# Two turns of layer-norm rows and one of combine weights done one head later in the second mixer

## What is computed

```python
x = x + L0_attn(layernorm(x))      # 16-head delta rule with short convolutions
x = x + L0_ffn(layernorm(x))       # 8 experts, top 2, plus a shared expert
x = x + L1_attn(layernorm(x))      # 16 query heads on 2 key/value heads, rotary, soft-capped, causal
x = x + L1_ffn(layernorm(x))       # 16 experts, top 6, combine weights from a softmax router
```

```python
logits = SOFTCAP * jnp.tanh((q @ k.T) * SCALE / SOFTCAP)
scores = jax.nn.softmax(jnp.where(causal, logits, -1e30), axis=-1)
out = scores @ v                   # then out @ Wo, added over the heads
```

## Time and profile before

| | |
|---|---|
| median of three runs | 869.14 us (868.95 to 869.23) |
| the profiled execution's own time | 869.01 us |
| its span (first to last instruction) | 867.2 us |
| TensorE matmul busy | 813.6 us, 94% of the span |
| VectorE busy | 456.9 us, 53% |
| ScalarE busy | 318.4 us, 37% |
| POOL busy | 161.9 us, 19% |
| mean granted TensorE clock | 0.988 |

### The profile page before, as it was taken

How to read it: one execution, slowest core, us unless ns; L and a number is a source line. 1 busy time by engine, 2 the same in 40 slices (tenths; PEclk the granted TensorE clock), 3 DMA queues, 4 the chain that set the end, 5 groups by cost and what they waited for, 6 DMA issues and landing times.

```text
span 867.2 us, 12754 instructions
## 1 busy us (share of the span) xinstructions
PE 813.6 (94%) x4543; PEld 568.6 (66%) x4543; DVE 456.9 (53%) x1054; ACT 318.4 (37%) x651; POOL 161.9 (19%) x256
## 2 busy tenths in 40 slices
PE   6979799889899977999999999998999999999998
PEld 3567566666567765677777776776766655555567
DVE  5999766757422225866464666476543252322223
ACT  3987777555033322443323243332312211111111
POOL 3652744113500070111111111111100000000000
PEclk9998999999999997999999999999999999999999
DMA  4002860281253230023010100100224344354431
GB/s 139 2 2 40 264 231 2 52 224 55 98 173 107 74 91 12 19 61 92 25 37 25 37 25 27 35 25 25 63 79 128 112 129 125 122 148 131 130 107 48
DMA packets 63957, 72.07 MB, mean 83 GB/s; under 512 B 14200, under 2 KB 48504, under 8 KB 63896
## 3 DMA queue, kind: packets, MB, share of 16 engines
q1 hardware_dynamic: 59048, 64.06, 24.8%
q0 software_dynamic: 1536, 4.20, 1.5%
q10 hardware_dynamic: 3312, 3.02, 1.0%
HBM read 55.45 MB, written 14.75 MB: 81 GB/s over the span
## 4 chain that ended last, share of the span: by engine, by line
PE 76%; DVE 10%; issue 5%; ACT 5%; another core or an unknown queue 1%; SPq 1%; DMA 1%; POOL 1%; DVEq 0%; ACTq 0%; POOLq 0%
PE bank L930 10%; PE bank L892 10%; PE bank L906 10%; PE bank L1107 8%; PE bank L1074 8%; PE bank L969 6%; PE bank L955 6%; PE bank L636 3%; PE bank L1857 3%; PE bank L658 2%; PE bank L1814 2%; PE bank L1841 2%; ACT arena L1914 1%; PE bank L979 1%; DVE sh L2395 1%
## 5 line engine op out<-in xcount | busy, mean ns | idle before, releaser
L1139 ACT ACTIVATE arena<-bank 128x512 f32<-128x512 f32 (+1 forms) x64 | 34.7, 544 | 230.0 <-PE bank L892 194.4
L1247 DVE TENSOR_TENSOR arena<-arena,bank 128x512 f32<-128x512 f32 (+1 forms) x47 | 30.7, 654 | 151.7 <-PE bank L906 151.7
L930 PE MATMUL bank<-arena 128*128 128x256 f32 x448 | 107.9, 382 | 1.4 <-DVE arena L1245 0.6
L892 PE MATMUL bank<-xnT,arena 128*128 128x512 f32 (+1 forms) x256 | 108.0, 544 | 0.5 <-issue 0.5
L906 PE MATMUL bank<-xnT,arena 128*128 128x512 f32 (+1 forms) x256 | 107.5, 543 | 0.0
L930 PEld LDWEIGHTS bank<-arena 128*128 128x128 f32 x448 | 85.2, 191 | 32.4 <-issue 20.6
L1208 ACT ACTIVATE arena<-bank 128x512 f32<-128x512 f32 (+1 forms) x96 | 46.8, 524 | 137.2 <-PE bank L1074 137.2
L855 POOL TENSOR_TENSOR arena<-arena,causal_t 128x256 f32<-128x256 f32 x64 | 45.0, 725 | 260.1 <-ACT arena L1213 260.1
L906 PEld LDWEIGHTS bank<-xnT,arena 128*128 128x128 f32 x256 | 49.2, 192 | 47.8 <-issue 45.9
L1107 PEld LDWEIGHTS bank<-arena 128*128 128x128 f32 x640 | 76.3, 191 | 4.4 <-POOL arena L855 2.9
L1107 PE MATMUL bank<-arena 128*128 128x129 f32 x640 | 77.0, 275 | 1.9 <-POOL arena L855 1.9
(11 more groups left out here) (236 smaller groups left out, 1173.2 us busy)
## 6 DMA issues: line engine op xcount, KB each, us to landing
arena<-in_w_gu SPq DMA_DIRECT2D x60, 256.0 KB, 3.6
rows_in<-place SPq DMA_DIRECT2D x5, 1664.0 KB, 14.2
arena<-in_w_dn SPq DMA_DIRECT2D x56, 128.0 KB, 3.6
arena<-in_wq SPq DMA_DIRECT2D x32, 128.0 KB, 2.2
arena<-in_wo SPq DMA_DIRECT2D x32, 128.0 KB, 2.0
arena<-cw_rows SPq DMA_DIRECT2D x15, 256.0 KB, 3.6
arena<-rows_in SPq DMA_DIRECT2D x23, 128.0 KB, 2.1
rows_out<-arena ACTq DMA_DIRECT2D x23, 128.0 KB, 1.7
```

What stands on the lines that cost most here:

```text
L892: mm = nc.tensor.matmul(ring(M)[0][:, 0:n], w_gu[:, slot_of(M), k * P:(k + 1) * P], xnT[:, k, cols], start=(k == 0), stop=(k == KD - 1))
L930: mm = nc.tensor.matmul(Y[s][half][l // 2][:, (l % 2) * DIM:(l % 2 + 1) * DIM], hh[:, M % 3, j * P:(j + 1) * P], w_dn[:, slot_of(M), :], s ...
L1139: nc.scalar.activation(sg[:, M % 2, 0:n], ring(M)[0][:, 0:n], ACT.Silu).then_inc(s_silu, 1)
```

## The change

Three turns move one pass on: the turn of norm group 8 from pass 21 to 22, of group 9 from 22 to 23, and of the combine weights from 28 to 29. With each go TensorE's wait for ScalarE's copy and that copy itself. Nothing is added or removed, and the streams of VectorE, POOL and SyncE are as they were.

```diff
@@ pe
-                if n == 21:
+                if n == 22:
                     self.ln_turn(pe, 8)
-                if n == 22:
+                if n == 23:
                     self.ln_turn(pe, 9)
                 if n == 24:
                     self.logits(pe, 2)
-                if n == 28:
+                if n == 29:
                     self.cw_turn(pe, 2)
...
-                if n == 21:
+                if n == 22:
                     pe.wait_ge(ln_xT, 4 + 9)
-                if n == 22:
+                if n == 23:
                     pe.wait_ge(ln_xT, 4 + 10)
                 if n == 24:
                     pe.wait_ge(s_sub, 3)
-                if n == 28:
+                if n == 29:
                     pe.wait_ge(s_cwT, 1)
```

## The result

The changed kernel is faster. Eight runs of it have a median of 865.99 us (863.07 to 870.01), beside 869.41 us (868.95 to 870.81) for eight of the kernel before. The ratio is 0.995, with a 95% interval of 0.9927 to 0.9973. A second set, six runs beside 22 of the kernel before, gave 864.27 and 869.71 us, ratio 0.9931 (0.9913 to 0.995). The sign is as forecast. The runs spread far more than the three that the forecast was made from: 7 us for the changed kernel, and 866.5 to 873.8 us over 63 runs of the kernel before. Where that comes from had to be found before the size of the gain could be told.

The account below looks back on a forecast made before the run. TensorE, busy for 94% of the span, was taken as the bound, so gains come where it pauses or runs slowly. Terms 1.64 + 0.19 + 2.18 + 0.16 + 1.69 = 5.86 us gave a forecast median of 863.3 us, range 862.6 to 865.2.

Parts of the forecast that it names:

- the two named ones: TensorE's waits at the turn of combine weights (L525, 2.2 us) and of norm group 8 (L437, 1.7 us).
- rival B: Mixer: a new wait replaces an old one, from late VectorE or ScalarE's copy; takes back at most 1.64 us; chance 0.07.
- rival D: Behind the mixer: late weight loads or combine rows lose the gain, time as before; chance 0.03.
- Terms 1 and 2: Passes 21 to 23: the pause at pass 21 goes, 1.64 us; the moved norm turn runs cheaper in the flow, 0.19.
- The check by starts: Pass 24's scores start at 559.7 instead of 561.55, given as 1.83 us, to confirm 1.64 + 0.19.
- Terms 3 and 4: Passes 28 and 29: the pause at pass 28 goes, 2.18 us; the combine weights' turn gets cheaper, 0.16; together 2.34.
- term 4: Turn of the combine weights: 0.60 us behind the pause, 0.44 in the flow of pass 29; gain 0.16.
- Term 5: Pass 28's scores: TensorE's clock no longer falls to half behind the pause, 2.16 us instead of 3.85; gain 1.69.
- the pause of 1.64 us: TensorE's pause in pass 21 before norm group 8's turn, followed by transposes with the clock at 1.00.
- Rival A: In or behind the mixer: a low-clock fall of the same length comes elsewhere; 865.0 us; chance 0.10.
- Rival C: TensorE's clock at new pass offsets: a fall lasting many sets of scores makes it slower, above 870.9 us; chance 0.02.

Follow-up runs that it names:

- that half alone: Only the two norm turns and their copies moved, against the kernel before; 866.59 us, ratio 0.9966 (0.9949 to 0.9982).
- the 4.7 us pause: The kernel before with VectorE's last ranking reduction (L508) done three times instead of once, lengthening the pause at pass 28; 872.45 us, ratio 1.0043.

## Why the prediction was right or wrong

**The bound and the direction: right.** Of the chain's pauses the two named ones went, no other took their place (rival B fell: 0.13 us of VectorE's room was enough), and what was won in the mixer reached the end (rival D fell: 0.2 us of waits behind it, as before).

**Terms 1 and 2: right.** 1.83 said, 1.9 measured with that half alone. (The check by starts adds up to 559.69, which makes the difference 1.86 and not 1.83; nothing hangs on it.)

**Terms 3 and 4: right in sum, one of them misnamed.** 2.34 said, 2.4 measured. The 0.16 us of term 4 belongs to the restart after the pause, not to the turn: with the pause kept and the turn moved, the scores paid it.

**Term 5: the step that failed.** Of bounds of 0 and 1.69 us it took the whole 1.69, "because no other row of the loop shows a fall", and so put a price that is paid now and then into the sum as one that is always paid. The size was right: where the fall happens it costs 1.6 to 1.7 us. But the fall happens in 3 of 5 traces of the kernel before, and in 3 of 7 with a pause of that length. The gain is therefore 5.9 us over an execution with the fall and 4.2 us over one without. The profile that the sum was made from happened to be one with it. The argument against chance was the spread of 0.28 us over three runs. Three runs cannot exclude something that happens about every second time, and 63 runs then spread over 7 us. The prediction gave two readings of the Trainium skill's page "TensorE: Matmul & The Clock Gate". By its Part 1 ("What's actually happening") the monitor runs free of the kernel. The traces agree in so far as the same instructions took 528.6 us with a fall and 527.0 without; that the place of the pause in the monitor's own time decides it, no run here shows. By its Part 4 transposes do not count as matmuls do. No run here settles that: the one trace with a pause and no transposes behind it had no fall, but neither had three others with a pause of the same length and the transposes.

The prediction held the pause of 1.64 us against chance, since the clock stayed at 1.00 behind it. In none of 8 traces did it fall there, so that row said something of shorter pauses and nothing of how often one of 2.2 us brings the fall.

**Rival A** had the right size and the wrong mechanism. The low clock did not reappear behind the mixer: in all three traces of the changed kernel the clock is at 1.00 from the first passes to the end. What made the gain smaller was that some executions before had never paid the 1.7 us. A chance of 0.10 for a result 1.7 us above the forecast was too low.

**Rival C** fell: no low stretch came with the new offsets.

**The range.** The first set's median, 865.99 us, lies 0.8 above its upper end, while its ratio applied to the 869.14 us that the forecast started from gives 864.8, inside, with an interval from 862.8 to 866.8. The range left out a spread that has nothing to do with the change: the part ahead of L938 took 337.7 to 344.7 us in the ten traces that have the long wait there, and with it alone the changed kernel runs from 862 to 869. Its median over all 14 timed runs is 865.2. The expectation from the traces is 4.2 us plus 1.65 in three of five executions, some 5.2 us; the two sets' medians gave 3.4 and 5.4.

## What to carry to other kernels

Work that feeds a later stage, and whose result is not needed for passes, should be placed on the critical engine where its input is surely there, since a wait in an in-order stream holds up everything behind it. Before counting a low-clock stretch as a term, take several traces of the same kernel: after a short pause (2.2 us here) it may be there in one and not in the next, so its price belongs in the range, times how often it occurs. Where total times spread by more than the effect, cut each trace at a row that the change does not touch and compare the parts.

## What had not been expected of the hardware

- The part ahead of L938 varies by itself. The changed kernel's second trace has the granted clock at 0.50 in five separate stretches before 250 us, its first in three, and starts the mixer 6 us later. How the time divides between those stretches and late arrivals was not tried.
- In the four traces from another chip that part took 328 to 333 us. There a wait ahead of the mixer was absent, and with it the low clock of some 10 us that the other traces have there. The chain of waits of the first changed trace has the wait, and the third, from that chip, has short work all along that place:

```profile
321.01 7.24 another core or an unknown queue
```

```profile
322.19 0.89 DVE x_sb L711 x2
324.49 1.28 ACT L1139
326.68 1.13 PE bank L930 x4
```

  What that wait is for (the row names an unknown queue; the program gathers rows by indirect DMA just there), and whether the chip or something else of those executions took it away, is open.
- A low clock costs less where part of it lies inside the pause. At the 4.7 us pause the clock was low for 6.8 us, and where TensorE is busy that costs 3.4; it cost 2.4, since it began at about 598.6, 1.9 us before the turn could start (600.52). It was still dearer than the falls at the 2.2 us pause, because the clock stayed low for longer: in the first trace of the kernel before it was low for 3.4 us (0.50 from 598 to 600, 0.64 from 600 to 602).
